# Routed mixture-of-experts tiles: scatter-adds of one expert's tiles may be in flight together, and row gathers run two tiles further ahead

## The reference

```python
x = L0_attn_x
x = x + attention(layernorm(x))          # 16 heads, fourth-degree polynomial, causal
x = x + ffn(layernorm(x))

def ffn(x):                               # 2048 tokens, 16 experts, 4 chosen per token
    w, sel = route(x, gate_weight, expert_bias)
    cw = (one_hot(sel, 16) * w[..., None]).sum(1)
    out = sum over e: cw[:, e] * (silu(x @ g[e].T) * (x @ u[e].T) @ d[e].T)
    return out + silu(x @ sg.T) * (x @ su.T) @ sd.T     # the shared expert
```

## Time and profile before

| | |
|---|---|
| median of 3 runs | 1170.63 us (1167.03 to 1176.07) |
| the profiled execution, its own time | 1174.09 us |
| its span in the trace | 1172.1 us |
| PE busy | 964.3 us (82%) |
| POOL busy | 524.0 us (45%) |
| DVE busy | 752.5 us (64%) |
| routed part, first scatter-add issued to last | 700.2 to 1164.5 us |

### The profile page before, as it was taken

How to read it: one execution, slowest core, us unless ns; L and a number is a source line. 1 busy time by engine, 2 the same in 40 slices (tenths; PEclk the granted TensorE clock), 3 DMA queues, 4 the chain that set the end, 5 groups by cost and what they waited for, 6 DMA issues and landing times. The chain is left out here.

```text
span 1172.1 us, 21004 instructions
## 1 busy us (share of the span) xinstructions
PE 964.3 (82%) x5770; PEld 457.7 (39%) x5771; DVE 752.5 (64%) x1663; ACT 563.5 (48%) x1009; POOL 524.0 (45%) x738
## 2 busy tenths in 40 slices
PE   5969998998779968866777998888888888788873
PEld 2433333343434424323534554444444344344431
DVE  2859975979987798588378655555555445444451
ACT  2348884897358764974243343333333333333330
POOL 0006663655336552774010035555555455555542
PEclk9988999999889889987779999999999999999996
DMA  8003335443324425844459867887878778777774
GB/s 324 29 36 105 113 108 179 145 144 109 111 89 145 145 72 183 322 145 164 135 171 320 308 212 181 183 188 183 186 192 195 166 183 193 167 171 181 178 178 64
DMA packets 76648, 193.48 MB, mean 165 GB/s; under 512 B 9904, under 2 KB 11056, under 8 KB 75312
## 3 DMA queue, kind: packets, MB, share of 16 engines
q1 hardware_dynamic: 58672, 149.53, 37.0%
q0 software_dynamic: 17920, 43.26, 20.6%
HBM read 131.67 MB, written 61.10 MB: 164 GB/s over the span
## 5 line engine op out<-in xcount | busy, mean ns | idle before, releaser
L746 PE MATMUL bank<-arena,xgT 128*128 (+1 forms) x1152 | 287.9, 387 | 3.5 <-ACT xgT L1033 3.1
L1069 POOL TENSOR_TENSOR s_p<-s_p,c_causal 128x128 f32<-128x128 f32 x256 | 148.5, 605 | 256.2 <-DVE s_p L1424 249.6
L485 PE MATMUL bank<-arena 128*128 128x512 f32 x384 | 187.8, 638 | 18.3 <-ACT arena L875 9.4
L1026 ACT ACTIVATE hT<-bank 128x512 f16<-128x512 f16 x96 | 57.3, 597 | 274.0 <-PE bank L756 266.3
L746 PEld LDWEIGHTS bank<-arena,xgT 128*128 128x128 f16 x1152 | 109.4, 100 | 133.6 <-issue 45.6
L1077 POOL TENSOR_TENSOR arena<-arena 128x768 f16<-128x768 f32 x68 | 115.0, 1691 | 97.2 <-ACT arena L824 97.0
L1113 POOL DMA_INDIRECT out<-yy,sidx x80 | 128.4, 1605 | 46.1 <-issue 43.2
L767 PE MATMUL bank<-wd,hT 128*128 128x512 f16 x576 | 148.2, 396 | 0.7 <-ACT hT L1026 0.7
L913 ACT ACTIVATE arena<-bank 128x512 f32<-128x512 f32 (+3 forms) x256 | 99.6, 440 | 84.7 <-PE bank L533 80.4
L1033 ACT ACTIVATE xgT<-bank 128x1024 f16<-128x1024 f16 x96 | 98.2, 1023 | 85.7 <-PE bank L737 84.4
L1696 DVE TENSOR_SCALAR yy<-bank,hsc 128x512 f32<-128x512 f32 x80 | 60.1, 751 | 123.3 <-DMA out<-yy,sidx 112.6
(11 more groups left out here) (172 smaller groups left out, 1426.7 us busy)
## 6 DMA issues: line engine op xcount, KB each, us to landing
wd<-w_scratch SPq DMA_DIRECT2D x82, 512.0 KB
arena<-w_experts SPq DMA_DIRECT2D x34, 768.0 KB, 5.9
w_scratch<-arena SPq DMA_DIRECT2D x34, 768.0 KB, 4.5
arena<-w_scratch SPq DMA_DIRECT2D x17, 1024.0 KB, 8.0
xin<-x SPq DMA_DIRECT2D x4, 1024.0 KB, 5.6
arena<-x SPq DMA_DIRECT2D x4, 1024.0 KB, 4.9
x_scratch<-arena SPq DMA_DIRECT2D x4, 1024.0 KB, 5.2
xg<-xn_scratch SPq DMA_DIRECT2D x16, 256.0 KB, 4.8
```

What stands on the lines that cost most here:

```text
L485: mm = pe.matmul(bk[:], xnT[:, c, m * P:m * P + P], wqkv[:, c, w * E:w * E + E], start=(c == 0), stop=(c == EC - 1))
L746: mm = pe.matmul(bank[2 + k][:], xgT[:, k, xh * EC + c, :], w, start=(c == 0 and xh + wh == 0), stop=(c == EC - 1 and xh == 1))
L1069: pool.tensor_tensor(d, d, C["causal"][:], ALU.mult).then_inc(p4_masked, 1)
```

## The change

Four things change together.

1. The semaphore `added` becomes two, one for even and one for odd routed tiles. Before `scatter` of routed tile n, POOL waits for the landing of all earlier tiles of its own parity (a constant), and of the other parity for a count that it loads from a new table `others_in` (`pool.value_load`, one register load per tile). The count is that of all earlier tiles of the other parity, or one less where tile n and tile n-1 belong to the same expert (and are no spare tiles). So tile n may be added while tile n-1 is in flight if they share the expert, since their tokens differ; it always waits for tile n-2. DVE makes the table once, with five small operations behind the tables of rows (`find_rows`), from a new constant `landed`.
2. `xg` has four buffers (`xg01`, `xg23`), with four semaphores.
3. `gather` in POOL's step t is that of tile t+2, not of tile t, and the numbers copied ahead are those of tile t+3. At the start four gathers go out ahead, where there were two.
4. POOL and PE take four routed tiles per turn of their loops, since the buffer number of `xg` has to be a constant. The semaphore `numbers` is split in two (`gather_no`, `scatter_no`). DVE's wait before it overwrites `yy` is for tile n-2 alone.

```diff
+def tile_pairs(eng, lo, hi, step, n=2):
+    with eng.Fori(0, (hi - lo) // n) as r:
+        for j in range(n):
+            step(Tile(r, lo + j, n))
...
+    c["landed"] = np.tile(16 * ((np.arange(RT)[None, :] + 1) // 2), (P, 1))
...
-        added = sem("added")
+        added = [sem("added_even"), sem("added_odd")]
...
             def weight_and_rows(t):
                 weight(t.plus(-2))
                 pool.wait_ge(weights_here, t.at(-1 - TB))
-                pool.wait_ge(numbers, t.at(-1 - TB) * 2 if not t.below(TB + 4) else t.at(2 - TB))
...
-                    gather_numbers(t.plus(1))
-                gather(t)
+                if t.r is not None or t.lo < NT - 3:
+                    pool.wait_ge(gather_no, t.at(3 - TB))
+                    gather_numbers(t.plus(3))
+                    gather(t.plus(2))
...
+            def landed(t):
+                n = t.plus(-TB)
+                if not t.below(TB + 3):
+                    others = pool.value_load(others_in[0:1, bass.ds(t.at(-TB), 1)], min_val=16, max_val=8 * RT)
+                    pool.wait_ge(added[1 - t.par], others)
+                elif not t.is_(TB):
+                    pool.wait_ge(added[1 - t.par], (n.lo + 1) // 2 * 16)
+                if not t.below(TB + 2):
+                    pool.wait_ge(added[t.par], n.uses(-1) * 16)
+
+            def add_rows(t):
+                landed(t.plus(-4))
+                pool.wait_ge(y_sb, t.at(-3))
+                pool.wait_ge(scatter_no, t.at(-3 - TB))
+                scatter_numbers(t.plus(-3))
+                scatter(t.plus(-4))
...
-                pool.wait_ge(y_sb, t.at(-3))
-                pool.wait_ge(added, t.at(-4 - TB) * 16)
-                scatter_numbers(t.plus(-3))
-                scatter(t.plus(-4))
...
-                    dve.wait_ge(added, t.at(-TB - 1) * 16)
+                    dve.wait_ge(added[k], t.plus(-TB).uses(-1) * 16)
```

More of the change, by code:

```diff
@@ L186, in build @@
         expert_id = sb("expert_id", [P, RT], I32)
+        others_in = sb("others_in", [P, RT], I32)
+        same = sb("same", [P, RT])
+        zero = sb("zero", [P, 1], I32)
         oh4 = sb("oh4", [P, MB * TOPK * NX])
@@ L295, in all_tiles @@
             tile_pairs(eng, FIRST, TB - 1, step)
-            for t in range(TB - 1, TB + 3):
+            for t in range(TB - 1, TB + n + 1):
                 step(Tile(None, t))
-            tile_pairs(eng, TB + 3, NT - 1, step)
-            step(Tile(None, NT - 1))
+            tile_pairs(eng, TB + n + 1, NT - n + 1, step, n)
+            for t in range(NT - n + 1, NT):
+                step(Tile(None, t))
         @block.sync
@@ L729, in gather_T @@
                 k = t.par
+                k4 = k if t.shared() else t.k4
                 if t.shared():
@@ L732, in gather_T @@
                 else:
-                    pe.wait_ge(xg_in[k], t.plus(-TB).uses() * 16)
+                    pe.wait_ge(xg_in[k4], t.plus(-TB).turns(4) * 16)
                 if not t.below(2):
@@ L1093, in weight, with gather_numbers @@
                 e = pool.value_load(expert_id[0:1, bass.ds(t.at(-TB), 1)], min_val=0, max_val=NX)
[L1094 removed]
+                pool.tensor_copy(wr[:, k:k + 1], xg[t.k4][:, E:XW].bitcast(F32)[:, bass.ds(e, 1)]
                                  ).then_inc(weights_here, 1)
[L1097 to L1100 removed]
+            def gather_numbers(t):
+                if not t.below(TB + 4):
+                    pool.wait_ge(xg_in[t.k4], t.plus(-TB).turns(4, -1) * 16)
+                pool.tensor_copy(gidx[:, t.k4:t.k4 + 1], row_id[:, bass.ds(t.at(-TB), 1)]).then_inc(gather_no, 1)
             def scatter_numbers(t):
[L1103 removed]
+                to = sidx[:, t.k4:t.k4 + 1]
+                if t.r is None:
+                    n = t.lo - TB
+                    pool.tensor_tensor(to, row_id[:, n:n + 1], zero[:], ALU.add).then_inc(scatter_no, 1)
+                else:
+                    pool.tensor_copy(to, row_id[:, bass.ds(t.at(-TB), 1)]).then_inc(scatter_no, 1)
             def gather(t):
[L1106 to L1107 removed]
+                k = t.k4
+                pool.indirect_dma_start(out=xg[k], out_offset=None, in_=xn_dram,
                                         in_offset=bass.IndirectOffsetOnAxis(ap=gidx[:, k:k + 1], axis=0)
@@ L1154, in _ @@
             pool.wait_ge(zeros_out, 16)
-            t = Tile(None, TB + 4)
-            weight_and_rows(t)
-            pool.wait_ge(y_sb, t.at(-3))
-            scatter_numbers(t.plus(-3))
-            scatter(t.plus(-4))
-            step(Tile(None, TB + 5))
-            tile_pairs(pool, TB + 6, NT - 2, step)
-            step(Tile(None, NT - 2))
-            step(Tile(None, NT - 1))
+            pool.wait_ge(others_known, 1)
+            for t in range(TB + 4, TB + 8):
+                step(Tile(None, t))
+            tile_pairs(pool, TB + 8, NT - 4, step, 4)
+            for t in range(NT - 4, NT):
+                step(Tile(None, t))
             for t in range(NT, NT + 4):
@@ L1167, in _ @@
                     weight(t.plus(-2))
+                landed(t.plus(-4))
                 pool.wait_ge(y_sb, t.at(-3))
-                pool.wait_ge(added, t.at(-4 - TB) * 16)
-                pool.wait_ge(numbers, RT + t.at(-2 - TB))
                 if t.below(NT + 3):
+                    pool.wait_ge(scatter_no, t.at(-3 - TB))
                     scatter_numbers(t.plus(-3))
                 else:
-                    gather_numbers(t.plus(-4), again=True)
+                    pool.wait_ge(scatter_no, RT)
+                    pool.tensor_tensor(gidx[:, 0:1], zero[:], zero[:], ALU.add)
                 scatter(t.plus(-4))
-            pool.wait_ge(added, 16 * RT)
+            for k in range(2):
+                pool.wait_ge(added[k], 16 * RT // 2)
         @block.vector
@@ L1626, in find_rows @@
                 dve.tensor_copy(row_id[:], free[:]).then_inc(ids_ready, 1)
+                dve.drain()
+                dve.tensor_copy(free[:], expert_id[:])
+                dve.drain()
+                dve.tensor_tensor(same[:, 1:RT], free[:, 1:RT], free[:, 0:RT - 1], ALU.is_equal)
+                dve.drain()
+                dve.scalar_tensor_tensor(out=same[:, 1:RT], in0=free[:, 1:RT], scalar=0.0, in1=same[:, 1:RT],
+                                         op0=ALU.is_gt, op1=ALU.mult)
+                dve.drain()
+                dve.scalar_tensor_tensor(out=same[:, 1:RT], in0=same[:, 1:RT], scalar=-16.0, in1=C["landed"][:, 1:RT],
+                                         op0=ALU.mult, op1=ALU.add)
+                dve.drain()
+                dve.tensor_copy(others_in[:, 1:RT], same[:, 1:RT]).then_inc(others_known, 1)
             def routing(t):
```

77 lines of the change are left out of this document (39 added, 38 removed).

## The result

| | before | changed |
|---|---|---|
| median | 1171.85 us (1167.03 to 1176.07, 4 runs) | **1110.43 us** (1109.14 to 1113.57, 4 runs) |
| ratio, 95% interval | | **0.9476** (0.9440 to 0.9512) |
| profiled execution, its span | 1174.09, 1172.1 us | 1111.27, 1109.4 us |
| first to last scatter-add | 464.3 us | 398.8 us |
| granted TensorE clock, mean | 0.928 | 0.931 |

The kernel is 5.2% faster: 61.4 us on the medians, 62.7 us on the two spans. The forecast of 1112 us is 1.6 us off. First the scatter-add line of the changed kernel, which answers to the earlier trace rows; the two lists are what POOL waited for ahead of it and who waited for its landing (us, times).

The account below looks back on a forecast made before the run. Bound: a chain of 80 scatter-adds, each waiting for the one before, 464.3 us. 58 x 4.85 + 21 x 5.88 = 404.8, plus 0.6 for the table, saves 58.9 us: 1112 us, range 1094 to 1148.

Parts of the forecast that it names:

- 58 steps freed, 21 serial: Routed part's 79 steps: 58 share an expert and may overlap; 14 changes of expert and 7 spare tiles stay serial.
- A freed step 4.85 us: Add-to-add step inside an expert: POOL 4.64, register load 0.05, DMA crowding 0.15; 4.66 to 5.3 us.
- rival (c): POOL, PE and DMA all reach their floor: freed steps 4.66, serial 5.7; 1097 us or a bit below; chance 0.04.
- A serial step 5.88 us: Step that still waits for the previous add's landing: the old mean, 5.7 to 6.4 us if weights fall into the add.
- The register load is hidden: POOL's new load runs while the gather's descriptors are made: 0.05 us a step, against 0.92 bare.
- rival (a): POOL becomes the bound as its register load isn't hidden: freed steps 5.56 us, 1153 us; chance 0.10.
- What is late next: Behind the chain of adds: POOL 4.64, PE 4.64, DMA 4.51 us per tile, capping a step's loss at 1.24 us.
- Lost time adds up at serial steps: A serial step sets POOL back 1.0 us, and almost nothing is won back between changes of expert.
- Gathers sooner are no second gain: Gathers two tiles ahead remove PE's 70.3 us of waits, but this adds nothing to the chain's gain.
- (b): Rival: DMA engines become the bound in the routed part; freed steps 5.3, serial 6.2 us; 1145 us; chance 0.12.
- (e): Rival: the table never lets a tile go early, or experts are cut otherwise; steps stay 5.88 us, 1171 us; chance 0.03.
- (d): Rival: adds in flight together disturb each other in DRAM; freed steps 6.3, serial 6.2 us; 1202 us; chance 0.03.

Follow-up runs that it names:

- e10: Changed kernel without overlap of adds and with gathers one tile ahead as before; register load, four buffers and loops of four stay: 1174.90 us, ratio 1.0011.
- e2: Changed kernel with overlap kept, but gathers late again, one tile ahead as in the kernel before: 1113.97 us, ratio 0.9506.
- e3: Changed kernel with 77 steps freed, adds going to rows that no neighbouring tile uses (output sums wrong): 1083.21 us, ratio 0.9245.
- e1: Changed kernel without overlap: each scatter-add waits for the one before; sooner gathers and all the rest stay: 1236.91 us, ratio 1.0537.
- e11: Changed kernel without overlap, gathers still sooner, and only half of the down weights loaded from the third tile on: 1192.86 us, ratio 1.0149.
- e5: Changed kernel with the register load of the table's count made twice for each tile: 1137.56 us, ratio 0.9717.
- e7: Changed kernel with four y buffers instead of two, so DVE waits for the landing of tile n-4: 1111.54 us, ratio 0.9443.
- e6: Changed kernel with the row numbers ahead of a scatter-add copied in the loop by an integer add of zero: 1114.71 us, ratio 0.9507.
- e4: Changed kernel with spare tiles freed too, on spare rows by parity, the row table made in 80 columns of constants: 1109.75 us, ratio 0.9449.

## Why the prediction was right, and where its terms were off

*The chain of adds is what bounded the kernel*: right. e10 against e2 puts nothing but the overlap between 1174.90 and 1113.97 us, and e3 takes the rest of the chain away but for the first two steps.

*58 steps freed, 21 serial*: two too many. The map of experts is right: POOL waits for a landing at each of its 14 changes. But the count took every step from the table, and the steps of routed tiles 1 and 2 wait by a constant: 56 are freed, 23 serial. By the prediction's own prices that is 2 x 1.03 = 2.1 us more.

*A freed step 4.85 us*: it is 4.68. The 0.15 us that I added for the DMA engines wasn't needed. They need 4.26 us a tile and not 4.51, and run at a share of 0.84; predicted was 0.85 to 0.92. Over 56 steps this term is 9.6 us too long, and its value would have been that of rival (c), 4.66.

*A serial step 5.88 us*: this term was mis-sized in two places that nearly cancel. At a change of expert it is 6.31 us, inside the bound of 6.4 that the prediction gave for the weights falling into the add. e1, e10 and e11 show what that collision costs in a chain that is serial throughout, and here the packets show weights and gathered rows beside the adds in question. Two of the 14 are of e1's kind, with a late start: 7.57 and 7.12 us, with the weights issued 0.03 and 0.28 us behind the add and its first data after 3.5 and 3.2 us. In the other twelve the add starts on time, within 0.2 us, and where the step is long its data moves for longer: 4.3 us ahead of the step of 7.31, against 2.35 on average before. How much of that is the weights' and how much the gather's isn't separated. At the end a step is 5.16 us and not 5.88. That isn't the overlap's doing: e10, without it, has 5.28 there. Numbers to issue takes 0.34 us in that code, which the prediction, not having the integer add on its list, took as 0.72, and the gathers are over. 14 x 0.43 - 7 x 0.72 = +1.0 us.

So the sum is 404.8 + 2.1 - 9.6 + 1.0 and 0.6 for the first two steps: 398.9. That 404.8 came within 6 us of 398.8 is in part luck: terms of -9.6, -5.0, +6.0 and +2.1 us offset one another, and most of the 6 us that were left was hidden by a first add 1.7 us later than predicted, by 0.5 us behind the last one, and by a median only 0.8 us below the profiled execution, where 3.5 had been carried over.

*The register load is hidden*: right for one load (1.00 to 1.09 us from gather to numbers, 1.05 to 1.15 predicted), and rival (a) falls. Its bare price was read too high, 0.92 for 0.6 to 0.75.

*What is late next*: POOL and PE at 4.64 us each is borne out by freed steps of 4.68; the DMA engines' 4.26 us stand 0.4 below. e5 shows that POOL has no room, e7 that the y buffers are not the pacer, and PE is busy 93% of the stretch, and 98% of it in e3. A faster POOL alone would gain little; that was not tried, since e6 made none.

*Lost time adds up at serial steps*: right. e3 gets back 27.2 us for 21 steps of the 23.

*Gathers sooner are no second gain*: right beside the overlap (e2), but for a reason that I had only in part. I had them at worst at zero. Alone they cost 5% (e1), since they take away the wait that kept the weights out of the add's flight. The overlap hides this, because a freed step doesn't wait for that landing.

*The waits*: PE's for gathers fell to 0 as predicted. POOL's for landings fell to 52 us (22.5 + 26.3 + 3.2), not to some 25. I had left out the waits of the first two steps (5.3 us), and that in the last tiles POOL has no gathers to do, and waits about 3 us where those in the loop wait 1.3.

*The table*: 0.60 us on PE, as worked out. *Weights covered*: PE never waits for them.

*Rivals (b) and (e)* fall with the step lengths. So does (d)'s time, but not its mechanism, whose case the kernel hardly reaches (e3). (c) had the freed steps right, 4.66 for 4.68, and needed serial ones of 5.7, which were 5.94.

## What to carry to other kernels

Where a wait keeps every transfer behind the one before, count how many of these orders the data really asks for, and put the condition into a table, loaded beside work that the engine does anyway: the gain is the number of freed steps times the distance to the next resource. Count the steps in the code too, with those written out ahead of a loop, and not in the data alone. Work out that resource's turn first (POOL's instruction by instruction, PE where nothing holds it, the DMA queues' share times the step), since it is the cap. And a wait that looks like pure loss may be what keeps two transfers apart: moving the gathers alone made this kernel 5% slower, so test each part of a change by itself before keeping it for its own sake.

## What was not expected of the hardware

- An add that is issued 0.33 us after the load of 512 KB of weights lands 5.8 us after its issue instead of 5.0. The two come by different queues, and still the add's data starts 0.6 us later, when most of the weights have gone. It is worst when the weights are issued 0.5 to 1.0 us behind the add: they get ahead of it all the same, and the add's first data comes 4.1 us after its issue (e1).
- Scatter-adds into different rows went out every 4.65 us for 77 steps in a row (e3) at no more engine time per tile, 4.24 us against 4.51 before, though each then needs 6.0 us to its last packet. Their data moves one after the other all the same.
- From the copy of the numbers to the issue of the add is 0.72 us in the loops and 0.34 us in some of the code written out behind them. In the kernel before, written-out code with a plain copy had 0.72 too (1134.02 to 1134.74), and in the loop the integer add of e6 has 0.71: neither the form nor the place makes the difference alone. Both together don't always bring it either: the written-out adds at the end of e4, which wait for no landing, have 0.65 to 0.69. The cause stays open.
- A second register load right behind one that is hidden beside a gather's descriptors costs 0.60 us a step.
